# A two-layer transformer tower on one core: VectorE empties the up-projection banks of the first layer's feed-forward, ScalarE applies Gelu in SBUF

## The reference, cut to what matters

```
xe = xf.reshape(MB, E, tpe, D)
h = jax.nn.gelu(jnp.einsum('metd,edf->metf', xe, w1) + b1[None, :, None, :], approximate=False)
y = jnp.einsum('metf,efd->metd', h, w2) + b2[None, :, None, :]
```

## Time and profile before

| | |
|---|---|
| three timed runs | 1319.59, 1322.98, 1324.32 us, median 1322.98 |
| the profiled execution | 1312.2 us, of which the span from the first to the last instruction is 1310.1 us |
| busy over the span | PE 82%, DVE 56%, ACT 37%, POOL 16% |
| mean granted TensorE clock | 0.902 of full |

### The profile page before, as it was taken

The page is one execution under the profiler, slowest core; times in us unless marked ns, Lnnn a source line. Parts: engine busy times, 40 slices in busy tenths (PEclk is TensorE's granted clock), DMA queues, the critical chain, the costliest instruction groups (busy, mean ns, idle before and its releaser), DMA issues. The chain is left out here.

```text
span 1310.1 us, 23297 instructions
## 1 busy us (share of the span) xinstructions
PE 1080.7 (82%) x8482; PEld 770.7 (59%) x8482; DVE 729.6 (56%) x1981; ACT 479.9 (37%) x970; POOL 212.1 (16%) x248
## 2 busy tenths in 40 slices
PE   1228997997999888889987899787898999999990
PEld 1224655543756355666455564574457999999990
DVE  7982445675534767646677456354552444444445
ACT  2111323445354443255543455251302333333332
POOL 3960000000000000200000200002022333333320
PEclk7558997989999899799977898698999999999995
DMA  5123150018522587021805130012941111111105
GB/s 168 18 57 136 48 195 17 17 54 149 57 73 78 218 192 81 33 73 65 157 5 65 66 105 1 1 65 69 378 158 32 42 33 42 34 41 37 38 29 196
DMA packets 73421, 108.90 MB, mean 83 GB/s; under 512 B 16592, under 2 KB 58336, under 8 KB 72864
## 3 DMA queue, kind: packets, MB, share of 16 engines
q1 hardware_dynamic: 66192, 74.75, 23.1%
q0 software_dynamic: 5280, 14.57, 3.4%
q10 hardware_dynamic: 1840, 18.10, 3.4%
HBM read 83.47 MB, written 40.97 MB: 95 GB/s over the span
## 5 line engine op out<-in xcount | busy, mean ns | idle before, releaser
L1688 DVE TENSOR_REDUCE mx<-scores_ps 128x4 f32<-128x1024 f32 (+1 forms) x160 | 187.0, 1169 | 124.3 <-PE scores_ps L1137 78.0
L1516 ACT ACTIVATE pt<-turned_ps 128x1024 f32<-128x1024 f32 (+1 forms) x160 | 158.0, 987 | 159.1 <-PE turned_ps L1159 111.1
L2222 PEld LDWEIGHTS x_ps<-x_xtT,x_w1s 128*128 128x128 f32 x1248 | 145.3, 192 | 3.4 <-ACT x_xtT L2250 1.5
L2222 PE MATMUL x_ps<-x_xtT,x_w1s 128*128 128x128 f32 x1248 | 145.8, 275 | 1.0 <-ACT x_xtT L2250 1.0
L2236 PE MATMUL x_ps<-x_experts,x_hT 128*128 x624 | 141.0, 379 | 0.0
L2236 PEld LDWEIGHTS x_ps<-x_experts,x_hT 128*128 128x128 f32 x624 | 115.6, 190 | 14.1
L1056 POOL COPY vpad<-v 128x64 f32<-128x64 f32 x64 | 13.2, 238 | 634.4 <-PE ps L1198 525.2
L1149 PE MATMUL turned_ps<-q,k 32*128 32x256 f32 x512 | 70.5, 352 | 27.5 <-DVE mx L1688 18.2
L1149 PEld LDWEIGHTS turned_ps<-q,k 32*128 32x128 f32 x512 | 43.0, 202 | 83.6 <-issue 44.6
L2265 ACT ACTIVATE x_hT<-x_ps,x_b1c 128x128 f32<-128x128 f32 x312 | 84.9, 382 | 16.9 <-issue 13.8
L2285 DVE COPY x_w1s<-x_experts 128x2048 f32 x39 | 55.2, 1418 | 49.5 <-PE x_ps L2222 37.8
(11 more groups left out here) (429 smaller groups left out, 1981.8 us busy)
## 6 DMA issues: line engine op xcount, KB each, us to landing
x_slots<-x_slots ACTq DMA_DIRECT2D x4, 4160.0 KB
wexp<-in_L_ffn_w SPq DMA_DIRECT2D x16, 1024.0 KB, 5.3
x_experts<-in_L_ffn_W SPq DMA_DIRECT2D x16, 1024.0 KB, 13.0
q<-heads SPq DMA_DIRECT2D x48, 128.0 KB, 5.3
k<-heads SPq DMA_DIRECT2D x48, 128.0 KB, 10.7
ha<-h SPq DMA_DIRECT2D x16, 256.0 KB, 3.2
x_pair<-y_rows SPq DMA_DIRECT2D x4, 1024.0 KB, 9.0
heads<-nat_k_hi SPq DMA_DIRECT2D x12, 256.0 KB, 4.0
```

Of the source, the lines that this page charges most:

```text
L1516: sc.activation(pt[v.index // 2 % (PT_RING // 2)][:, :, 0:wide], turned_ps[:, :, 0:wide], ACT.Exp)\
L1688: v.tensor_reduce(mx[:, u.group % 2, 0:blocks, u.n:u.n + 2].rearrange("p b n -> p n b"), scores_ps[:, :, 0:blocks * (P if u.causal else T) ...
L2222: last = mm(ps[2 * (i % 2) + f // KH][:, f % KH * P:(f % KH + 1) * P], w1s[:, i % 2, c, f * P:(f + 1) * P], xtT[:, i % 2, c, :], start=c = ...
```

## The change

VectorE gets a new instruction at the end of each up slot. It copies the raw products of the bank (128x512) into `hid` and so frees the bank. ScalarE then applies bias and Gelu to `hid` in place, still four ACTIVATEs between two table loads, and waits for the copies. The down products wait for a new semaphore, `hidden`, which counts finished Gelu blocks. The figures of the slots say so too: each up slot now has .7 us of DVE, the ACT figure is 3.2 instead of 4.5, and the `+1` marks are gone.

```
-                [(1.75, 0, 0, True, f"up{e}0+1"), (1.75, 0, 4.5, False, f"up{e}1"), (1.75, 0, 0, False, f"up{e}2+1"),
-                 (1.75, 0, 4.5, False, f"up{e}3"), (.9, 0, 0, True, f"down{e}0+1"), (.9, 1, 0, False, ""),
+                [(1.75, .7, 0, True, f"up{e}0"), (1.75, .7, 3.2, False, f"up{e}1"), (1.75, .7, 0, False, f"up{e}2"),
+                 (1.75, .7, 3.2, False, f"up{e}3"), (.9, 0, 0, True, f"down{e}0+1"), (.9, 1, 0, False, ""),
...
-        if name[0:2] in ("up", "vg") or name in ("o0", "o1"):
+        if name[0:2] == "vg" or name in ("o0", "o1"):
             return 2, 0
...
                         if bb == 0 and f % 2 == 0:
-                            evicted(f"up{e}{f // 2}", p)
+                            pe.wait_ge(sg("hidden"), (E_IT * p + e) * FT0 + f + 2)
...
-                            bank = full(f"up{e}{m}", p)
+                            added(act, f"up{e}{m}", p)
                             for i in range(2):
                                 f = 2 * m + i
-                                sc.activation(hid[:, e, f, :], bank[:, i * T:(i + 1) * T], ACT.Gelu,
+                                sc.activation(hid[:, e, f, :], hid[:, e, f, :], ACT.Gelu,
                                               bias=b1c[:, (E_IT * p + e) * FT0 + f:(E_IT * p + e) * FT0 + f + 1])\
-                                    .then_inc(sg("y_act_b"), 1)
+                                    .then_inc(sg("hidden"), 1)
...
+                    v.tensor_copy(hid[:, e, 2 * n:2 * n + 2, :], full(f"up{e}{n}", p)[:, :]
+                                  .rearrange("p (f t) -> p f t", f=2)).then_inc(sg("y_dve_b"), 1)
                     yield
```

## The result

The changed kernel takes 1308.99 us (median of 5, 1305.55 to 1313.31) against 1322.98 us (median of 5, 1319.59 to 1325.2). The ratio is **0.991**, 95% interval 0.9886 to 0.9935: 14.0 us less by the medians, outside the 0.5% band. The profiled execution took 1305.55 us with a span of 1303.5 us; that of before had a span of 1310.1 us. So the two profiles are only 6.6 us apart.

What follows compares the result with a forecast made beforehand. TensorE was taken to bound the changed stretch, so only its idle time could be won: -8.2 +1 +0.5 -6.5 +2 = -11.2 us, 1312.2 to about 1301 profiled, 1312 us timed with 10.8 us carried over; range 1301 to 1327.

Steps and rivals of the forecast that it cites:

- The bank wait: Up products of pairs 0 and 1: TensorE's waits for Gelu to free a bank all go, -8.2 us.
- Y1a of pairs 0 and 1 shorter by 4 us each: Sign that the forecast is right: this stretch of pairs 0 and 1 shortens by 4 us in each.
- 32 copies at 0: VectorE's added copies, 22 us of work in the up slots, cost nothing beside TensorE; +22 us if all exposed.
- ScalarE's late batches: Gelu batches end later by waiting for the last copy, delaying the Exp: +1 us, ends 0 and +13.
- The wait of the earlier trace: Pair 1 at 572.57 us: the down product's wait for a bank behind Gelus and an Exp stays 2.2 us.
- Gelu out of SBUF: ScalarE's 64 Gelus take 530 ns instead of 472: 3.7 us more, mostly covered, so +0.5 us, ends 0 and +7.4.
- The end of the loop: Pair 3: Y1b starts earlier as down products follow at once, -6.5 us; the gate's second part pays back +2 us.
- From the profile to the median: Whole kernel: timed median lies 10.8 us above the profiled execution, carried over from about 1301 to 1312 us.
- One gain is lost on the way: Rival, chance 0.20: removed stalls return in Y1b or the loop's end gains nothing; -3 to -6 us, 1317 to 1320.
- VectorE and ScalarE become late: Rival, chance 0.10: copies delay the maxima, Gelus and Exp; 1326 us with half exposed, 1343 with all.
- Far memories: Rival, chance 0.05: Gelu's SBUF price of 7.4 us and VectorE's PSUM price on 32 copies are exposed; 1322 us.
- More than forecast: Rival, chance 0.05: the shift also removes pair 1's 2.2 us wait and gives a fuller clock; about 1302 us.

Runs made afterwards that it cites:

- E5: The changed kernel's new slot order without the copies, Gelu reading the up banks in PSUM as before: 1311.83 us, ratio 0.9912 to the kernel before.
- E10: The new slot order without the copies timed a second time, beside the changed kernel on one chip: 1313.22 us, ratio 0.9943 to the kernel before.
- E1: The changed kernel's copies and Gelu in SBUF, but with the old slot figures and so the old order: 1325.76 us, ratio 1.0033 to the kernel before.
- E8: The changed kernel with each of the 32 copies done twice, order unchanged: 1316.39 us, ratio 0.9938 to the kernel before.
- E6: The changed kernel without the five filler products of pair 3, behind the loop: 1310.84 us, ratio 0.9895 to the kernel before.
- E4: The changed kernel again, unaltered, on another chip: 1305.53 us, ratio 0.9891 to the kernel before.
- E9: The changed kernel once more, its order replayed, beside the order without copies on one chip: 1307.62 us, ratio 0.9907 to the kernel before.
- E7: The changed kernel with one batch of eight Gelus per expert instead of two of four, slot figures and order following: 1337.55 us, ratio 1.0112 to the kernel before.
- E3: The changed kernel with the old order up to x slot 160 and its new order from there: 1315.82 us, ratio 0.9951 to the kernel before.
- E2: The changed kernel with its new order up to x slot 160 and the old order from there: 1318.6 us, ratio 0.9963 to the kernel before.

## Why the prediction was right, and where it was not

The forecast was 1312 us with a range of 1301 to 1327; 1308.99 us came. The total was right and its division was not, so there is luck in how near it came. In the profiles the forecast gave -6.7 us to the loop and -4.5 us to the end; -10.2 us and +0.6 us came, and 3.0 us more ahead of the loop, where the change does nothing.

**The bank wait, -8.2 us by the copies.** The wait did go, all of it. But the step gave to the copies what the order had mostly done: without them 2.8 us are left (E5, E10), and in the old order the copies remove the whole wait and are 3.2 us slower than before (E1). The order rows ahead of the prediction already showed it for pair 0, where `q0` no longer stands between `up02` and `up03`. The prediction drew nothing from that row. The changed loop is 10.2 us shorter than before in the profiles, 2 us more than the wait itself; 7.1 us of that are idle time, the rest is clock. The sign "Y1a of pairs 0 and 1 shorter by 4 us each" did not come: in pair 0 it took 59.0 us from the first up to the last down product and takes 59.6 us now, in pair 1 53.4 and 50.6 us. The new order places other slots among these products, so the stretch is not a measure of the wait.

**32 copies at 0.** This was wrong as a general statement. The prediction looked behind a copy for the next maximum only. In the old order the row scale of pair 2 stands behind three of them, with 5.90 us of idle TensorE at one place (E1). In the new order TensorE has down products to do in that time. A second dose of copies costs some 5 us (E8), so the first one is probably not free either; that this is its price is inferred, not shown.

**ScalarE's late batches, +1 us.** Nothing contradicts it, and nothing here could show so small a term. TensorE's idle time ahead of L1149 is now

```profile
L1149 PE MATMUL turned_ps<-q,k 32*128 32x256 f32 x512 | 70.4, 351 | 28.5 <-DVE mx L1688 19.3
```

against 27.5 us; in E6 and E4, with the same order, it is 26.5 and 29.5 us. The wait of the earlier trace rows did not stay at 2.20 us; it is 3.17 us (at 569.95 us).

**Gelu out of SBUF, +0.5 us.** The size was off: I took 530 ns, it is 498 ns on average, 26 ns more than out of PSUM. That is 1.7 us over 64 Gelus instead of 3.7 us. By the table of the Trainium skill ("VectorE: DVE Perf Modes", "The TRN2 errata") it would have been 43 ns more each, an estimate of 2.8 us; the direction agrees, the size is less here. The 690 against 586 ns that the prediction set beside this rule compare VectorE with ScalarE on the same copy, not two memories on one engine, so they bear little on it.

**The end of the loop, -6.5 us and +2 us.** Half right. Y1b of pair 3 starts 49.5 us behind the first up product of its Y1a, against 53.6 us before (908.96 - 855.37): -4.1 us. The missing 2.4 us are fillers: I took 4.4 us for them, and they took 6.79 us, most of it at the lower clock. The trace of before already had 6.42 us for the ten rows (902.09 to 908.51); the earlier trace rows shows four of them. The payback of +2 us is there as computed: L1904 starts 11.9 us behind those transposes, straight behind the gate's L2039, where L1902 started 9.8 us behind them, and the first L1416 comes 20.3 us behind them (918.02 - 897.70) where it was 18.5 us (927.5 - 908.96). What I had not counted is another 2.9 us behind that, in the low stretch at 920 to 930 us. Together the end is 0.6 us longer, not 4.5 us shorter. With the order alone it is 6 us longer than before, and 3.9 to 5.5 us longer than with the copies. 2.1 us of the gap to the changed kernel lie within the up products of pair 3 (851.6 to 877.7 us in E10, 848.2 to 872.2 us in the changed kernel), 0.9 us of them a wait for Gelu; the rest was not traced.

**From the profile to the median.** -11.2 us was computed for the profiled execution, where 6.6 us came; in the medians it is 14.0 us (13.3 us in E9, 17.1 us in E4). The rule of carrying over the difference of profile and median hid an error of some 5 us, because the profiled execution of before was a short one, and 3.0 us of it are the later start of the loop. Whether its end of 132.5 us is typical of its kernel is open; with one profile of before it can't be told.

Of the rivals, none came as described. *One gain is lost on the way* holds for the place (the end gained nothing), but the loop gave more than forecast. *VectorE and ScalarE become late* is what E1 shows: the mechanism is real, it just needed the old order. *Far memories* did not come: a copy took 691 ns, a Gelu 498 ns, and the kernel gained all the same. *More than forecast* did not either, as the wait of the earlier trace rows grew. The low end of the range, 1301 us, does not follow from the terms named for it: 1322.98 less 14.7 (8.2 and 6.5) less 3 is 1305 us.

## What to carry to other kernels

A change that also alters a scheduler's figures is two changes. Time the new mechanics in the old order and the old mechanics in the new order before giving the gain to either: here they are worth +3 us and about -9 us alone, and about -15 us together, by the medians. A copy that frees a buffer early is put into the queue of an in-order engine and waits there for its producer. What costs time is not the copy but what stands behind it, so look for the longest chain of that engine, not for the next instruction. And before a few us are read from the length of a stretch in two profiles, profile one kernel more than once: the same loop took 487.8 to 495.8 us here. Its idle time spread less.

## What the runs showed of the hardware

- TensorE's clock is a term of its own. The ten rows of the five fillers took 6.79 us in the changed kernel, with the granted clock at 0.50 from 890 to 895 us, and 4.46 us in E7, where they came straight behind products and the clock was 1.00. 0.50 is the lower of the two levels, 1.2 GHz. In the changed kernel TensorE had idled for 2.61 us up to 883.79 us; the clock was still 1.00 from 880 to 885 us. It then idled for 2.79 us up to 887.67 us, and from 885 to 890 us the mean clock was 0.54.
- The same order can meet it at different places. The 32 products of L1416 in Y1b of pair 3 took 394 ns in the median in the changed kernel, E3, E4, E5 and E10 (416 ns in E9), all with the new order at the end, and 270 ns in the kernel before, E1 and E2. But E1 and E3, with the same instructions in the same order up to the end of the loop, needed 498.0 and 503.8 us for it, while TensorE was idle for 58.5 and 56.5 us. E3 had the low level where E1 did not:

```profile
490.00:500.00 10.00, 10.00 (x64) 7.59 (x67) 1.84 (x3) 4.74 (x8) 0.00 (x0) 0.50 0.02 4
535.00:545.00 10.00, 10.00 (x66) 7.12 (x64) 7.63 (x35) 2.31 (x5) 0.00 (x0) 0.50 0.01 2
```

  E1's clock was 1.00 and 0.76 in these two windows. That is the noise under which a few us of a single profile should be read.
- A Gelu on 128x256 elements costs 472 ns out of PSUM and 498 ns out of SBUF, in place.
